# Rotary attention on one Trainium2 core: a unit's second maxima ahead of its second scores on TensorE

## The chip, the cores and the metric

The kernel runs on one core of a Trainium2 chip. The metric is the device time of one execution in microseconds (us). TensorE does the matrix products, VectorE the reductions and elementwise work on them, ScalarE the exponentials and copies, GpSimd smaller elementwise work, and SyncE starts the transfers. Each engine takes its own instructions in order; semaphores hold an instruction until what it needs is there.

## The reference

Two blocks of attention, each followed by a gated feed-forward block, all on layer-normed input and added to it: x has 16 batches of 512 tokens with 128 features. The first attention is causal, the second rotary and not causal. Both have 16 heads of width 8.

```python
x = x + attn_a(layernorm(x))        # causal
x = x + ffn(layernorm(x))
x = x + attn_b(layernorm(x))        # rotary
x = x + ffn(layernorm(x))

# attn_b
q, k = rope(q, k)
scores = einsum('bhnd,bhmd->bhnm', q, k) / sqrt(d)
attn = softmax(scores, axis=-1)
out = einsum('bhnm,bhmd->bhnd', attn, v)
```

## The kernel before

There are four stages with barriers between them: causal attention, feed-forward, rotary attention, feed-forward. The change touches only the program of TensorE inside `attention` (lines 773 to 787), and only what it does for the rotary stage.

Attention is a pipeline over batches, with steps n from -1 to 19. In step n the queries, keys and values of batches n+1 and n are projected, the row maxima of the scores of batch n-1 are found, the scores of batch n-2 are made again with the maxima subtracted and put through the exponential, and the weighted values of batches n-2 and n-3 and the output projection of batch n-4 are done. Scores and maxima of both kinds meet in the 15 steps from n = 2 to n = 16.

A step is 16 units u. A unit holds four score matrices of 128 keys by 512 queries, two for each of two pairs of heads:

- `scores(n, u, 0)` and `scores(n, u, 1)` (line 681) are two matmuls each, one on the lower and one on the upper half of the rows, into the banks of `ps_score`. ScalarE reads each bank with an exponential (line 662) and writes `b_prob`.
- `maxes(n, 2u)` and `maxes(n, 2u+1)` (line 695) are two matmuls each, into two of the four banks of `ps_max`. VectorE reduces the two banks to negated maxima in one instruction (line 577).
- `weigh` (line 716) multiplies the probabilities of the unit two before with the values: four products into `ps_out`. ScalarE copies the output of a group of four units to `b_o_raw` (line 635).
- `misc_work` holds what comes once in a step: the projections of keys (in unit 0), turned keys (2), values (4), output (6), queries (11) and turned queries (13) into `ps_max` (lines 733, 769, 745), and into `ps_score` the turned maxima (1 and 10, line 725) and the turned input (9, line 753). VectorE and ScalarE take the results out in the unit after.

Banks go round in a fixed order that is worked out from the lists `act_turns` and `dve_turns`. `ps_score` has three banks: a score may start when the exponential of the score three turns earlier has read its bank (`act_bank_free`). In a unit without other work the second matmul of the first scores so waits for the first exponential of the second scores of the unit before. `ps_max` has two pairs of banks: maxima may start when VectorE has read what was put there two turns earlier (`dve_banks_free`). Where another projection has taken a turn, the next unit's first maxima wait for the second reduction of this unit, not for the first.

VectorE works through its list in order too: in the unit after a projection it takes that result out before the unit's two reductions. The statistics of the normalisation (lines 180, 184) stand ahead of the reductions of unit 6, the reciprocals and the output projection's sum (lines 607, 613) ahead of those of unit 7, the normalised input (line 202) ahead of those of unit 8.

Of the kernel before, what the change touches and what calls it, by code (L numbers as in the profile page):

```python
# [55 lines left out]
def count(per, b, more=0):  # L56

    return per * b + more


def wait(eng, sem, value):

    if isinstance(value, int) and value <= 0:
        return
    eng.wait_ge(sem, value)
# [141 lines left out]
def attention(nc, sem, m, a, tag, causal):  # L207
# [3 lines left out]
    rotary = not causal  # L211
# [37 lines left out]
    def width(j):  # L249

        return P * j if causal else 0

    def on(n, lag):

        return 0 <= n - lag < B
# [23 lines left out]
    def dve_banks(name, k=0):  # L279

        i = 2 * (dve_at[name, k] % 2)
        return m["ps_max"][:, i:i + 2]
# [26 lines left out]
    def dve_banks_free(pe, n, name, k=0):  # L309

        before = turn_before(dve_turns, 2, n, dve_at[name, k])
        if before is None:
            return
        name, b, k = before
        if name == "max":
            pe.wait_ge(s["max"], count(MAXES, b, k + 1))
        elif name == "proj":
            pe.wait_ge(s["resid"], b + 1)
        elif name == "v":
            pe.wait_ge(s["v"], b + 1)  # L320
        elif name in ("qr", "kr"):
            pe.wait_ge(s[name[0] + "_turn"], b + 1)
        else:
            pe.wait_ge(s[name + "_main" if rotary else name], b + 1)
# [10 lines left out]
    with own, nc.Block() as block:  # L335
# [195 lines left out]
        def _(dve):  # L531
            dve.wait_ge(s["loads"], 80 if rotary else 64)

            def split_weights():

                dve.wait_ge(s["w_raw"], 16 * len(W_PIECES))
                for i, (_, name, cols) in enumerate(W_PIECES):
                    at = slice(W_AT[name], W_AT[name] + cols)
                    full = raw(i).rearrange("p k f -> p (k f)")
                    dve.tensor_copy(m["w_hi"][:, at], full).then_inc(s["w_hi"], 1)  # L540
                    dve.wait_ge(s["w_hi"], i + 1)
                    dve.tensor_tensor(m["w_lo"][:, at], full, m["w_hi"][:, at].bitcast(F32), ALU.subtract)\
                        .then_inc(s["w_lo"], 1)
                    dve.wait_ge(s["w_lo"], i + 1)
                    dve.tensor_reduce(m["w_rest"][:, i:i + 1], m["w_lo"][:, at].bitcast(F32), AX.X, ALU.max,
                                      apply_absolute_value=True).then_inc(s["w_rest"], 1)
# [119 lines left out]
        def _(pe):  # L666
            pe.wait_ge(s["loads"], 80 if rotary else 64)

            def scores(n, u, half):

                b, c = n - 2, (n - 2) % STACKS
                G, j = u // T, u % T
                p, lo = 2 * G + half, width(j)
                if half == 0 and u % (UNITS // 2) == 0:
                    h = u // (UNITS // 2)
                    pe.wait_ge(s[f"aug{h}"], count(32, b, 32))
                for o in range(2):
                    k = 4 * u + 2 * half + o
                    rows = slice(SIDE * o, SIDE * o + KROWS + AUG)
                    act_bank_free(pe, n, "score", k)  # L680
                    pe.matmul(act_bank("score", k)[:, 0:S - lo], m["stack_k"][c][rows, p, P * j:P * (j + 1)],  # L681
                              m["stack_q"][c][rows, p, lo:S], start=True, stop=True).then_inc(s["score"], 1)

            def maxes(n, k):

                b, c = n - 1, (n - 1) % STACKS
                p, t = k // T, k % T
                if k == 0:
                    pe.wait_ge(s["stack_q"], count(LOADS, b, LOADS))
                    pe.wait_ge(s["stack_k"], count(LOADS, b, LOADS))  # L690
                dve_banks_free(pe, n, "max", k)
                to, keys = dve_banks("max", k), P * (t + 1) if causal else S
                for o in range(2):
                    rows = slice(SIDE * o, SIDE * o + KROWS)
                    last = pe.matmul(to[:, o, 0:keys], m["stack_q"][c][rows, p, P * t:P * (t + 1)],  # L695
                                     m["stack_k"][c][rows, p, 0:keys], start=True, stop=True)
                if causal:
                    for o in range(2):
                        last = pe.matmul(to[:, o, keys - P:keys], m["mask_q"][:], m["ident_b"][:],  # L699
                                         start=False, stop=True, skip_group_check=True)  # L700
                last.then_inc(s["max_ps"], 1)

            def weigh(b, u):

                G, j = u // T, u % T
                if u == 0:
                    pe.wait_ge(s["v_aug"], b + 1)
                if j == 0:
                    wait(pe, s["o_raw"], count(GROUPS, b, G))
                if causal:  # L710
                    pe.wait_ge(s["masked"], count(UNITS, b, u + 1))
                else:
                    pe.wait_ge(s["prob"], count(4 * UNITS, b, 4 * u + 4))
                lo = width(j)
                for g in range(4):
                    last = pe.matmul(m["ps_out"][32 * g:32 * g + HD + 1, lo:S], m["v_aug"][b % 2][:, j, 4 * G + g, :],  # L716
                                     m["prob"][u % PROBS][:, g, lo:S], start=(j == 0), stop=(j == T - 1),
                                     skip_group_check=True)
                last.then_inc(s["pv"], 1)
# [53 lines left out]
            for n in range(-1, STEPS):  # L773
                for u in range(UNITS):
                    if on(n, 2):
                        scores(n, u, 0)
                    if on(n, 1):
                        maxes(n, 2 * u)
                    if u < 2 and on(n, 3):
                        weigh(n - 3, UNITS - 2 + u)  # L780
                    if u >= 2 and on(n, 2):
                        weigh(n - 2, u - 2)
                    if on(n, 2):
                        scores(n, u, 1)
                    if on(n, 1):
                        maxes(n, 2 * u + 1)
                    misc_work(n, u)

# [332 lines left out]
```

## Time and profile before

| what | value |
|---|---|
| time, median of 3 runs (lowest to highest) | 2466.25 us (2465.03 to 2470.92) |
| time of the profiled execution | 2471.75 us |
| its span, from the first to the last instruction | 2470.0 us |
| granted TensorE clock over the span | 0.94 of full speed |
| TensorE busy (matmuls), share of the span | 2097.5 us, 85% |
| VectorE busy | 1723.2 us, 70% |
| ScalarE busy | 1482.2 us, 60% |
| rotary attention, 1238 to 2065 us: busy TensorE, VectorE, ScalarE | 715.03, 683.70 and 592.56 us of 827 |

A busy time is the sum over an engine's instructions, overlaps counted once. In a row of the timeline, the start and the duration of one group of neighbouring instructions of a kind are given (x2 is two of them), and in brackets how long the engine had been idle and what it waited for. Matmuls are pipelined, so a pair can show 0.39 us while the next pair starts 0.22 us after it.

### The profile page before, as it was taken

What the parts mean: (1) busy time and instruction counts of PE and PEld (TensorE: products, weight loads), DVE (VectorE), ACT (ScalarE), POOL (GpSimd) and SP (SyncE); (2) the same over time, 40 slices, a digit from 0 to 9 for tenths busy, and PEclk for the clock granted to TensorE, in tenths of its full rate; (3) what the DMA queues carried; (4) which work ended last, traced back from release to release, by engine and by line L of the source; (5) the groups of instructions that cost most, each with busy time, mean ns of one, the idle gap of its engine ahead of it and who ended that gap; (6) DMA issues with size and microseconds to landing.
All of it is one profiled execution on the core that took longest, in us unless ns stands there. A gap on an engine that the chain in (4) does not pass through costs nothing. (4 is left out here: it accounts for less than half of the span.)

```text
span 2470.0 us, 37314 instructions
## 1 busy us (share of the span) xinstructions
PE 2097.5 (85%) x13378; PEld 971.9 (39%) x13378; DVE 1723.2 (70%) x2590; ACT 1482.2 (60%) x2980; POOL 982.3 (40%) x1184
## 2 busy tenths in 40 slices
PE   0799999999985999998378898989898885999998
PEld 0233333333322777776112222222222112777776
DVE  5677777777643667664388889888988843666663
ACT  0166666666662655655037777777777773655655
POOL 2355555555421544544322332233323101554544
PEclk8599999999985999999569999999999997999999
DMA  5535454545310000000433344334433300000000
GB/s 155 108 78 103 83 106 88 105 85 106 67 21 11 1 1 1 1 1 2 101 77 62 68 86 87 68 67 88 85 70 65 64 16 11 9 9 14 13 10 18
DMA packets 99853, 136.48 MB, mean 55 GB/s; under 512 B 20560, under 2 KB 81488, under 8 KB 93520
## 3 DMA queue, kind: packets, MB, share of 16 engines
q1 hardware_dynamic: 99664, 134.02, 26.0%
q8 instruction: 111, 1.82, 0.3%
q14 instruction: 78, 0.64, 0.1%
HBM read 67.91 MB, written 55.57 MB: 50 GB/s over the span
## 5 line engine op out<-in xcount | busy, mean ns | idle before, releaser
L577 DVE TENSOR_REDUCE b_negmax<-ps_max 128x2 f32<-128x1024 f32 x512 | 614.2, 1221 | 92.9 <-PE ps_max L695 91.5
L662 ACT ACTIVATE b_prob<-ps_score 128x512 f32<-128x512 f32 x1024 | 545.8, 599 | 206.7 <-PE ps_score L681 205.5
L662 ACT ACTIVATE a_prob<-ps_score 128x512 f32<-128x512 f32 (+3 forms) x1024 | 384.0, 437 | 226.0 <-PE ps_score L681 224.0
L577 DVE TENSOR_REDUCE a_negmax<-ps_max 128x2 f32<-128x256 f32 (+3 forms) x512 | 411.4, 822 | 150.1 <-PE ps_max L699 142.6
L681 PE MATMUL ps_score<-b_stack_q,stack_k 50*128 50x512 bf16 x1024 | 258.8, 387 | 56.8 <-ACT b_prob L662 48.3
L716 PE MATMUL ps_out<-b_prob,b_v_aug 128*9 128x512 f32 x2048 | 268.6, 596 | 17.7 <-ACT b_o_raw L635 11.6
L978 PE MATMUL ps_score<-fb_h,w_hi 128*128 128x512 f32 x1024 | 252.0, 401 | 29.7 <-DVE fb_h L892 28.7
L978 PE MATMUL ps_score<-fa_h,w_hi 128*128 128x512 f32 x1024 | 251.4, 400 | 29.7 <-DVE fa_h L892 28.7
L494 POOL TENSOR_SCALAR_AFFINE_SELECT a_prob<-a_prob 128x512 f32<-128x512 f32 x256 | 162.0, 635 | 276.8 <-ACT a_prob L662 276.8
L695 PE MATMUL ps_max<-stack_k,b_stack_q 48*128 48x512 bf16 x1024 | 231.1, 397 | 27.1 <-DVE b_negmax L577 17.3
L681 PEld LDWEIGHTS ps_score<-b_stack_q,stack_k 50*128 50x128 bf16 x1024 | 63.9, 93 | 417.8 <-ACT b_prob L662 337.3
L978 PEld LDWEIGHTS ps_score<-fb_h,w_hi 128*128 128x128 f32 x1024 | 193.3, 190 | 82.7 <-DVE fb_h L892 36.6
L978 PEld LDWEIGHTS ps_score<-fa_h,w_hi 128*128 128x128 f32 x1024 | 193.0, 190 | 82.4 <-DVE fa_h L892 36.6
L716 PE MATMUL ps_out<-a_prob,a_v_aug 128*9 128x512 f32 (+3 forms) x2048 | 195.9, 456 | 27.3 <-ACT a_o_raw L635 17.1
L681 PE MATMUL ps_score<-a_stack_q,stack_k 50*128 50x512 bf16 (+3 forms) x1024 | 199.4, 315 | 9.7 <-ACT a_prob L662 6.4
L695 PE MATMUL ps_max<-stack_k,a_stack_q 48*128 48x128 bf16 (+3 forms) x1024 | 173.5, 312 | 17.8 <-DVE a_negmax L577 10.6
L452 POOL TENSOR_TENSOR b_qf<-b_qf,b_turned 128x512 f32<-128x512 f32 x32 | 40.6, 1268 | 356.4 <-DVE b_turned L565 356.4
L681 PEld LDWEIGHTS ps_score<-a_stack_q,stack_k 50*128 50x128 bf16 x1024 | 63.0, 93 | 230.2 <-ACT a_prob L662 124.8
L699 PE MATMUL ps_max<-ident_b,mask_q 128*128 128x128 bf16 x1024 | 150.8, 231 | 0.0
L846 POOL TENSOR_TENSOR fb_h<-fb_h2f,fb_h 128x512 fp32r<-128x512 f32 x64 | 82.6, 1290 | 144.5 <-ACT fb_h L931 144.5
L846 POOL TENSOR_TENSOR fa_h<-fa_h2f,fa_h 128x512 fp32r<-128x512 f32 x64 | 82.6, 1290 | 144.0 <-ACT fa_h L931 144.0
L202 DVE TENSOR_SCALAR xhat<-x,mv,rstd 128x128 f32<-128x128 f32 x256 | 112.4, 501 | 19.2 <-POOL rstd L194 19.2
(139 smaller groups left out, 2877.1 us busy)
## 6 DMA issues: line engine op xcount, KB each, us to landing
stack_k<-d_stack SPq DMA_DIRECT2D x64, 384.0 KB, 6.0
d_stack<-a_parts SPq DMA_DIRECT2D x64, 192.0 KB, 2.8
a_stack_q<-d_stack SPq DMA_DIRECT2D x32, 384.0 KB, 5.7
d_stack<-b_parts SPq DMA_DIRECT2D x64, 192.0 KB, 2.8
b_stack_q<-d_stack SPq DMA_DIRECT2D x32, 384.0 KB, 5.6
d_stack<-a_parts SPq DMA_DIRECT2D x64, 128.0 KB, 2.8
d_stack<-b_parts SPq DMA_DIRECT2D x64, 128.0 KB, 2.8
d_stack<-a_parts SPq DMA_DIRECT2D x64, 64.0 KB, 2.5
```

What stands on the lines that cost most here:

```text
L202: last = dve.tensor_scalar(m["xhat"][:, t, :], m["x"][:, b, t, :], m["mv"][:, t, 0:1], m["rstd"][:, t:t + 1], ALU.subtract, ALU.mult)
L452: pool.tensor_tensor(m["qf"][:, i], m["qf"][:, i], m["turned"][:, i], ALU.add).then_inc(s[name], 1)
L494: pool.affine_select(out=tri, in_=tri, compare_op=ALU.is_ge, fill=0.0, base=0, pattern=[[0, 4], [1, P]], channel_multiplier=-1).then_inc(s ...
L577: dve.tensor_reduce(m["negmax"][:, t, :, p], dve_banks("max", k)[:, :, 0:keys], AX.X, ALU.max, negate=True).then_inc(s["max"], 1)
L662: act.activation(m["prob"][u % PROBS][:, g, lo:S], act_bank("score", 4 * u + g)[:, 0:S - lo], ACT.Exp).then_inc(s["prob"], 1)
L681: pe.matmul(act_bank("score", k)[:, 0:S - lo], m["stack_k"][c][rows, p, P * j:P * (j + 1)], m["stack_q"][c][rows, p, lo:S], start=True, st ...
L695: last = pe.matmul(to[:, o, 0:keys], m["stack_q"][c][rows, p, P * t:P * (t + 1)], m["stack_k"][c][rows, p, 0:keys], start=True, stop=True)
L699: last = pe.matmul(to[:, o, keys - P:keys], m["mask_q"][:], m["ident_b"][:], start=False, stop=True, skip_group_check=True)
L716: last = pe.matmul(m["ps_out"][32 * g:32 * g + HD + 1, lo:S], m["v_aug"][b % 2][:, j, 4 * G + g, :], m["prob"][u % PROBS][:, g, lo:S], sta ...
L846: pool.tensor_tensor(h[k][:, 1, f], hf[k][:, f % 2], h[k][:, 0, f], ALU.subtract)\
L978: mm = pe.matmul(to, w[:, cols], moving(part), start=first and i == 0, stop=last and i == len(pairs) - 1)
```

## The change

In TensorE's loop over units the call that makes the second maxima of a unit moves, for the rotary stage, ahead of the call that makes the second scores. In the causal stage the order stays. Everything else is as before.

```diff
                     if u >= 2 and on(n, 2):
                         weigh(n - 2, u - 2)
+                    if rotary and on(n, 1):
+                        maxes(n, 2 * u + 1)
                     if on(n, 2):
                         scores(n, u, 1)
-                    if on(n, 1):
+                    if causal and on(n, 1):
                         maxes(n, 2 * u + 1)
                     misc_work(n, u)
```

## Rows read from the trace of the kernel before

**Rows 1.** Busy time by engine (start:end, us, then PE to POOL, clock, DMA).
```profile
1565.20:1614.70 49.50, 44.54 (x292) 10.96 (x292) 44.20 (x52) 37.07 (x71) 14.93 (x20) 1.00 0.38 77
```

**Rows 2.** Waits in the same step: total us, times, longest.
```profile
PEld ps_score L681 <- ACT b_prob L662: 20.6, 29, 0.9
...
DVE b_negmax L577 <- PE ps_max L695: 5.4, 17, 0.7
...
PE ps_score L681 <- ACT b_prob L662: 2.6, 7, 1.0
```

**Rows 3.** Timeline of TensorE, unit 12 into unit 13, no other work.
```profile
1603.72 1.05 PE L716 MATMUL ps_out<-b_prob,b_v_aug 128*9 128x512 f32 x8
1604.69 0.39 PE L681 MATMUL ps_score<-b_stack_q,stack_k 50*128 50x512 bf16 x2
1604.92 0.38 PE L695 MATMUL ps_max<-stack_k,b_stack_q 48*128 48x512 bf16 x2
1605.14 0.38 PE L681 MATMUL ps_score<-b_stack_q,stack_k 50*128 50x512 bf16 x1
1605.77 0.39 PE L681 MATMUL ps_score<-b_stack_q,stack_k 50*128 50x512 bf16 x1 [0.25 <-ACT b_prob L662]
1605.77 0.60 PE L695 MATMUL ps_max<-stack_k,b_stack_q 48*128 48x512 bf16 x2
1606.30 1.05 PE L716 MATMUL ps_out<-b_prob,b_v_aug 128*9 128x512 f32 x8
```

**Rows 4.** Timeline of VectorE and ScalarE in that unit.
```profile
1603.91 1.22 DVE L577 TENSOR_REDUCE b_negmax<-ps_max 128x2 f32<-128x1024 f32 x1
...
1605.35 2.36 DVE L577 TENSOR_REDUCE b_negmax<-ps_max 128x2 f32<-128x1024 f32 x2 [0.22 <-PE ps_max L695]
...
1605.12 2.06 ACT L662 ACTIVATE b_prob<-ps_score 128x512 f32<-128x512 f32 x4 [0.49 <-PE ps_score L681]
```

**Rows 5.** Timeline, unit 11 with the projection of the queries into unit 12.
```profile
1601.69 0.38 PE L695 MATMUL ps_max<-stack_k,b_stack_q 48*128 48x512 bf16 x2
1602.00 1.13 PE L733 MATMUL ps_max<-b_xT,b_weights 128*128 128x512 f32 x2
1603.06 0.39 PE L681 MATMUL ps_score<-b_stack_q,stack_k 50*128 50x512 bf16 x2
1603.40 0.39 PE L695 MATMUL ps_max<-stack_k,b_stack_q 48*128 48x512 bf16 x2
...
1602.11 1.23 DVE L577 TENSOR_REDUCE b_negmax<-ps_max 128x2 f32<-128x1024 f32 x1 [0.29 <-PE ps_max L695]
```

**Rows 6.** Timeline, unit 6 with the statistics and the output projection.
```profile
1584.37 0.86 DVE L180 BATCH_NORM_STATS2 stats<-x 128x6 f32<-128x128 f32 x4
...
1585.56 2.32 DVE L577 TENSOR_REDUCE b_negmax<-ps_max 128x2 f32<-128x1024 f32 x2
...
1586.90 1.13 PE L745 MATMUL ps_max<-b_weights,b_oT 128*128 128x128 f32 x8 [0.69 <-DVE b_negmax L577]
```

**Rows 7.** Timeline, unit 1 with the turned maxima into unit 2.
```profile
1570.43 1.08 ACT L662 ACTIVATE b_prob<-ps_score 128x512 f32<-128x512 f32 x2 [0.49 <-PE ps_score L681]
1571.40 0.57 ACT L627 ACTIVATE b_nm_rows<-ps_score 16x512 bf16<-16x512 bf16 x1
1571.87 0.57 ACT L635 ACTIVATE b_o_raw<-ps_out 128x512 f32<-128x512 f32 x1
...
1572.54 1.04 PE L716 MATMUL ps_out<-b_prob,b_v_aug 128*9 128x512 f32 x8 [0.37 <-issue]
```

**Rows 8.** Timeline, units 8 and 9 behind the normalised input; group output of unit 14.
```profile
1592.28 4.62 DVE L577 TENSOR_REDUCE b_negmax<-ps_max 128x2 f32<-128x1024 f32 x4
...
1593.14 0.39 PE L681 MATMUL ps_score<-b_stack_q,stack_k 50*128 50x512 bf16 x1 [0.25 <-ACT b_prob L662]
1593.57 0.39 PE L695 MATMUL ps_max<-stack_k,b_stack_q 48*128 48x512 bf16 x2
...
1608.68 0.60 ACT L635 ACTIVATE b_o_raw<-ps_out 128x512 f32<-128x512 f32 x1
```

## The prediction, made before the change was run

> **What bounds the kernel now.** I read the page first for where the time lies, then the 16 units of one step of the rotary attention (49.50 us, the same from step to step), first by engine, then by who waits for whom, then in order of time. In that step TensorE is busy for 44.54 us, VectorE for 44.20 and ScalarE for 37.07 [rows 1]. No engine is full, so the length of a step must come from a chain that goes over several engines. Two waits are candidates. VectorE waits 17 times for the maxima, 5.4 us in all; TensorE waits 7 times for ScalarE's exponentials before a score, 2.6 us, and its weight loads 29 times, 20.6 us [rows 2]. The change helps the first kind, and I must see what it does to the second.
>
> The unit without other work shows it [rows 3, 4]. The probabilities are weighed from 1603.72, the second scores start at 1604.69 (0.97 later), ScalarE takes up their exponential at 1605.12 (0.43 later), and the second matmul of the next unit's first scores, which writes the bank that this exponential reads, starts at 1605.77 (0.65 later). The next weighing starts at 1606.30, another 0.53 later. The sum 0.97 + 0.43 + 0.65 + 0.53 = 2.58 us is the distance from weighing to weighing, with nothing left over. So this unit is held by a loop: weighing, second scores, exponential, bank free, next first scores, weighing. I call it the score loop. VectorE sits beside it: it starts its reductions at 1603.91 and 1605.35, and after a start it could begin the next 1.13 us later (two back to back take 2.36, one 1.23) [rows 4]. It waits for the second maxima and doesn't set the pace here.
>
> **What the change moves.** Nothing is added or taken away: the same two matmuls per unit, with their bank wait, now stand before the second scores instead of behind them, in the 15 steps that have both (one batch's scores, the next batch's maxima). No DMA, no instruction of another engine and no bank assignment changes. The moved wait is for the reduction of the unit before, or for the operation that takes out another result; both ended long before the weighing does (the reduction begun at 1603.91 ends at 1605.14, its bank is next wanted after 1606.3) [rows 4], so I price it at nothing. If it were late, the second scores would now be queued behind it, and ScalarE behind them.
>
> *The score loop gets longer.* From the start of the second scores to the start of the second maxima it is 0.23 us [rows 3]. In the new order that time lies between the weighing and the second scores, in the middle of the loop. TensorE's idle time later in the unit can't give it back, because that idle time is itself the wait for the exponential, which has moved by the same 0.23. So a unit held by the score loop goes from 2.58 to 2.81 us. How many are there? Of the 7 waits of matmuls for exponentials, six are this pattern (0.25 us each) and one is the step's first score (1.0) [rows 2, 3]. Three more boundaries, behind the turned maxima and the turned input, have the same chain with one more ScalarE operation in it: two exponentials from 1570.43, row of maxima at 1571.40, output of a group at 1571.87, and the next weighing at 1572.54 waits for that [rows 7]. That is ten. One of them doesn't count: behind the normalisation the first maxima wait for VectorE's reduction (started at 1592.28, over at 1593.51) until 1593.57, while the score that waited for the exponential starts at 1593.14: 0.43 us of slack [rows 8]. A second is unit 5, ahead of the output projection, which is taken with it below. Eight remain: 8 x 0.23 = +1.84 us in a step.
>
> *Units held by VectorE get shorter.* Here another result is computed at the unit's end, and the next first maxima wait until the second reduction has left the bank. In the unit with the projection of the queries the reduction starts at 1602.11 and the first maxima at 1603.40, 1.29 later; the first scores had started at 1603.06 and need 0.22 of TensorE, so 0.12 us is waiting [rows 5]. The second maxima come 0.23 sooner after the weighing, the reduction too (its 0.22 of idle time goes, and VectorE was free); but TensorE, busy with scores, can use only 0.12. Four units are of this kind (keys, turned keys, values, queries): -0.48. For the turned queries nothing: with the wait gone the next weighing waits for the output of a group, which ScalarE starts at 1608.68 behind the last exponential [rows 8], and that is 0.23 later now.
>
> *Statistics and output projection.* Behind the second reduction of unit 5 stand the statistics (from 1584.37), then two reductions from 1585.56, and the projection at 1586.90 waits for the first of them, 0.69 us idle [rows 6]. That is one chain of VectorE over two units. It starts with a reduction that the change frees by 0.22, so two units together shorten by 0.22. TensorE reaches the projection only about 0.2 later than before, inside the 0.69.
>
> The sum for a step: 1.84 - 0.48 - 0.22 = +1.14 us. The last two of the 15 steps lack the queries of a next batch; I count them like the others. 15 x 1.14 = 17 us. The profiled execution then goes from a span of 2470.0 to 2487.0 and from 2471.75 to 2488.75 us; the median of the runs shown is 5.5 below that execution, so 2466.25 + 17 = 2483 us, +0.7%.
>
> The one term that the trace of before does not show is what a pair of maxima costs between a weighing and a pair of scores. Below: nothing, if it ran beside the weighing's tail or the scores; it can't gain. Above: 0.31 us, the distance from the second maxima to the next kind of matmul (1601.69 to 1602.00) [rows 5]. I take 0.23, the distance between a pair of scores and the pair of maxima behind it, since both are pairs of matmuls of 512 columns on the two halves of the rows [rows 3]. The ends give 15 x (0 - 0.70) = -10 and 15 x (8 x 0.31 - 0.70) = +27 us: 2456 to 2493.
>
> **Rivals.** *VectorE sets the pace (faster).* If the score loop had slack that I don't see, the reductions would come sooner and everything would follow. For it: VectorE is busy for 89% of the step and has 5.4 us of idle time in front of the maxima, 0.22 us of it in front of the second reduction of the plain unit [rows 1, 2, 4]. If the 0.22 went in all 16 units, that would be 15 x 16 x 0.22 = 53 us: 2413. In the small form only the units held by VectorE gain and the loop costs nothing: -10 us, 2456. The small form is the likelier of the two. It decides for the change if the second score's bank is free without the exponential's being late. Against it: the loop closes to 0.01 us [rows 3, 4]. The Trainium skill ("Perfetto Trace Analysis", Optimization Strategy) tells one to take the most contended engine, find the gaps on it and make what they wait for start sooner. By occupancy, with TensorE's judged otherwise, that engine is VectorE, and this change does what the rule asks; by that rule the time would fall. The rows of the score loop speak against it.
>
> *The loop takes only half (no change).* If the pair of maxima overlaps the scores behind it by half, a step changes by 8 x 0.12 - 0.70 = +0.3 us, 4 us in all: 2470. The trace shows for pairs only full distances of 0.22 to 0.23, against it.
>
> *It takes more (slower still).* If the weight loads of the second scores no longer hide, 0.31 in the eight loops, and none of the 0.70 is given back because the exponential then holds those units too, it is 15 x 8 x 0.31 = 37 us: 2503. Against it: where another result is computed, TensorE works for 1.06 us between the second maxima's 0.31 and the next scores [rows 5], which is longer than the 0.65 from exponential to score.
>
> *It changes nothing* because the order isn't what the text says: the loop in the code is plain, 1%, taken into the rival of no change.
>
> **How the numbers follow.** Within 0.3% (7.4 us, about what a measurement of this kernel can tell from no change) is 2458.9 to 2473.6. My forecast, 2474 to 2495 around 2483, has 0.73; the half cost 0.12; the faster rival 0.09 (part of its small form lies under 2458.9, part in the band; I leave 0.08 faster and put 0.01 in the band); slower still 0.06. So faster 0.08, same 0.13, slower 0.79. The range leaves out 0.17: the faster rival, some of the band and most of the slowest; 2466 to 2496.
>
> **What the profile after would show.** In the unit without other work: weighing, maxima 0.97 later, second scores at 1.20, exponential at 1.63, next weighing at 2.81. The step at 50.6 to 50.7 us instead of 49.50, VectorE's busy time as before (44.2) and its idle time larger, though the wait in front of the second reduction is smaller and now stands in front of the first. ScalarE's wait for the scores grows by about 1 us a step. The unit pair with the statistics is shorter by 0.2. The other three stages and their times are the same. The prediction is wrong if the plain unit stays at 2.58 (the pair hides), or if the weighings' distances in units with other work don't fall.

## The result, and the profile after

In the first four runs the changed kernel took 2490.74 us (median, 2488.13 to 2494.15) and the kernel before 2465.64 us; the ratio is 1.0097, 95% interval 1.0083 to 1.0112. Six more runs against 23 of the kernel before (below) give 1.0074, 1.0057 to 1.0092: 18 us slower. I had forecast 2483 us and 17 us slower; the interval of the first four runs (20 to 28 us) leaves that out, the later one (14 to 23 us) holds it. The profiled execution took 2489.67 us with a span of 2487.9 us, 17.9 us over the span before.

One step of the rotary attention in the kernel after, by engine, and its waits (us in total, times, longest). The stretch is again one step, from the first score of a batch to that of the next.

```profile
1574.80:1625.40 50.60, 43.92 (x292) 10.88 (x293) 44.78 (x51) 36.96 (x71) 14.94 (x20) 1.00 0.37 75
```

```profile
ACT b_prob L662 <- PE ps_score L681: 13.6, 22, 0.8
...
DVE b_negmax L577 <- PE ps_max L695: 5.1, 9, 0.9
PE ps_score L681 <- ACT b_prob L662: 4.8, 9, 1.3
```

The clock is at 1.00 and the busy times are those of [rows 1] within 0.62 us. VectorE's rose from 44.20 to 44.78, though one reduction takes 1221 ns in the mean as before (1222). VectorE waits for maxima 9 times where it waited 17 times, and yet as long as before, 5.1 us against 5.4 [rows 2]. The change removed VectorE's wait in front of the second maxima in most units, and the time came back in longer waits in front of the first. TensorE's matmuls wait for exponentials 4.8 us where it was 2.6 [rows 2].

Units 12 and 13, the stretch of [rows 3], on TensorE, and then VectorE and ScalarE in unit 12 as in [rows 4]:

```profile
1613.72 1.05 PE L716 MATMUL ps_out<-b_prob,b_v_aug 128*9 128x512 f32 x8
1614.69 0.39 PE L695 MATMUL ps_max<-stack_k,b_stack_q 48*128 48x512 bf16 x2
1614.92 0.59 PE L681 MATMUL ps_score<-b_stack_q,stack_k 50*128 50x512 bf16 x3
1615.99 0.39 PE L681 MATMUL ps_score<-b_stack_q,stack_k 50*128 50x512 bf16 x1 [0.47 <-ACT b_prob L662]
1615.99 0.60 PE L695 MATMUL ps_max<-stack_k,b_stack_q 48*128 48x512 bf16 x2
1616.52 1.05 PE L716 MATMUL ps_out<-b_prob,b_v_aug 128*9 128x512 f32 x8
```

```profile
1613.95 2.40 DVE L577 TENSOR_REDUCE b_negmax<-ps_max 128x2 f32<-128x1024 f32 x2
...
1616.63 2.53 DVE L577 TENSOR_REDUCE b_negmax<-ps_max 128x2 f32<-128x1024 f32 x2 [0.28 <-PE ps_max L695]
...
1615.34 2.06 ACT L662 ACTIVATE b_prob<-ps_score 128x512 f32<-128x512 f32 x4 [0.59 <-PE ps_score L681]
```

The two reductions of the unit now stand back to back (one row, x2, from 1613.95), so the wait of 0.22 us inside the pair is gone; in its place VectorE waits 0.28 us ahead of the next pair. ScalarE's exponential starts 1.62 us after the weighing (1.40 before), TensorE idles 0.47 us for it and not 0.25, and the next weighing comes after 2.80 us, not 2.58.

The output projection, as in [rows 6], and the next weighing behind the turned maxima, as in [rows 7]:

```profile
1593.83 0.86 DVE L180 BATCH_NORM_STATS2 stats<-x 128x6 f32<-128x128 f32 x4
...
1596.36 1.13 PE L745 MATMUL ps_max<-b_weights,b_oT 128*128 128x128 f32 x8 [0.25 <-DVE b_negmax L577]
...
1581.55 0.57 ACT L635 ACTIVATE b_o_raw<-ps_out 128x512 f32<-128x512 f32 x1
...
1582.22 1.05 PE L716 MATMUL ps_out<-b_prob,b_v_aug 128*9 128x512 f32 x8 [0.37 <-issue]
```

The projection's wait fell from 0.69 to 0.25 us. In unit 2 the weighing still follows the copy of the output by 0.67 us, so it moved with it.

### The profile page after: what moved, and what is told of

It reads as the page before. It is cut to its first block and busy times, and to the rows that moved or that the text cites. A ratio compares the mean times of both kernels' runs of the same rounds, so it can differ in the third digit from the quotient of the medians.

```text
span 2487.9 us, 37314 instructions
## 1 busy us (share of the span) xinstructions
PE 2090.7 (84%) x13378; PEld 971.6 (39%) x13378; DVE 1731.7 (70%) x2590; ACT 1480.7 (60%) x2980; POOL 982.4 (39%) x1184
## 5 line engine op out<-in xcount | busy, mean ns | idle before, releaser
L577 DVE TENSOR_REDUCE b_negmax<-ps_max 128x2 f32<-128x1024 f32 x512 | 616.5, 1221 | 97.1 <-PE ps_max L695 89.9
L681 PE MATMUL ps_score<-b_stack_q,stack_k 50*128 50x512 bf16 x1024 | 240.6, 383 | 90.7 <-ACT b_prob L662 84.7
L695 PEld LDWEIGHTS ps_max<-stack_k,b_stack_q 48*128 48x128 bf16 x1024 | 51.4, 94 | 252.9 <-issue 108.7
```

Source lines behind the costliest of these rows:

```text
L577: dve.tensor_reduce(m["negmax"][:, t, :, p], dve_banks("max", k)[:, :, 0:keys], AX.X, ALU.max, negate=True).then_inc(s["max"], 1)
```

## The experiments

All lengths of a step below are the distance between the first scores of two steps in one profile. In the kernels before and after these rows are:

```profile
1565.26 0.39 PE L681 MATMUL ps_score<-b_stack_q,stack_k 50*128 50x512 bf16 x2 [1.04 <-ACT b_prob L662]
...
1614.76 0.39 PE L681 MATMUL ps_score<-b_stack_q,stack_k 50*128 50x512 bf16 x2 [1.05 <-ACT b_prob L662]
```

```profile
1574.83 0.39 PE L681 MATMUL ps_score<-b_stack_q,stack_k 50*128 50x512 bf16 x2 [1.26 <-ACT b_prob L662]
...
1625.42 0.39 PE L681 MATMUL ps_score<-b_stack_q,stack_k 50*128 50x512 bf16 x2 [1.26 <-ACT b_prob L662]
```

That is 49.50 and 50.59 us.

**The change timed again (change_again).** The first four runs stood 25 us apart by their medians, the steps explain 17.6.

> The change itself, timed in more rounds to see whether the median moves as far as the steps do. The profile of the changed kernel has 50.59 us for a step against 49.50, 17.6 us over the 15 steps. If the score loop explains all of it, the median difference is 17 to 18 us (ratio 1.007). If something outside the rotary steps is slower too, it is 21 to 28 us (1.0083 to 1.011) as in the first four runs, and the profile must show it in another stage.

Measured: 2488.29 us (6 runs) against 2469.83 (23 runs), ratio 1.0074, 1.0057 to 1.0092, 18 us. The steps are 50.59 us again. From the first score of step 2 to that of step 17 it is 757.5 us here and 759.3 in the first profile of the changed kernel, against 741.7 in the kernel before: 15.8 and 17.6 us. So the steps account for the change within about 2 us. The first four runs had, by chance, the kernel before 4 us under its median here and the changed kernel 2 us over.

The 1.8 us between the two profiles are in the first of the 15 steps (53.25 and 51.45 us), which isn't like the others. TensorE's granted clock was still 0.50 of full speed, its lower level (1.2 GHz), for the first 5 to 15 us of it in all profiles. In both_ends below this lasted 5.5 us and the step took 47.78 us, 0.2 more than the next; in loop_again it lasted 14.5 us and the step took 54.76 us, 4.0 more than the next. Sums over the 15 steps of two profiles carry this difference, the distances of the steps behind it don't.

**Only where VectorE holds TensorE (only_held).** From the kernel before:

```diff
+                    early = rotary and u in (0, 2, 4, 5, 7, 11)
+                    if early and on(n, 1):
+                        maxes(n, 2 * u + 1)
                     if on(n, 2):
                         scores(n, u, 1)
-                    if on(n, 1):
+                    if not early and on(n, 1):
                         maxes(n, 2 * u + 1)
```

> The second maxima go ahead of the second scores only in units 0, 2, 4, 5, 7 and 11, whose reduction releases something that TensorE or VectorE waits for. Score loop theory: the loop isn't lengthened where it binds, the gains stay: 3 x 0.12 + 0.09 + 0.22 (unit 5, through the statistics) + 0.20 (unit 7, through the normalised input) = 0.87 us a step, a step of 48.6, 13 us faster in all (2453). Rival, a pair of maxima ahead of scores costs TensorE time wherever it stands: 6 x 0.23 = 1.4 us a step slower or, less the gains, 0.5 slower.

Measured: 2462.67 us (12 runs), ratio 0.9977, 0.9963 to 0.9991: 6 us faster. The step:

```profile
1558.54 0.39 PE L681 MATMUL ps_score<-b_stack_q,stack_k 50*128 50x512 bf16 x2 [1.05 <-ACT b_prob L662]
...
1607.38 0.39 PE L681 MATMUL ps_score<-b_stack_q,stack_k 50*128 50x512 bf16 x2 [1.05 <-ACT b_prob L662]
```

That is 48.84 us, 0.66 less than before and not 0.87. The missing 0.2 is unit 7: from its weighing to that of unit 8 it grew from 2.59 to 2.81, and from unit 8 to unit 9 it fell from 2.80 to 2.59. The score loop took what the normalised input gave. The other terms came as written. The steps give 9 us, the runs 6; the last experiment bears on the rest.

**Only where the score loop holds (only_loop).** The same edit with units (1, 3, 9, 10, 12, 14, 15).

> The second maxima go ahead of the second scores only in units 1, 3, 9, 10, 12, 14 and 15, where the next unit waits for the exponential of the second scores. Score loop theory: 7 x 0.23 = 1.6 us a step slower and nothing gained, a step of 51.1, 24 us slower in all (2490): more than the whole change costs. Rival, VectorE sets the pace: no slower than before, since its waits in front of the second reductions shrink in these units too.

Measured: 2504.04 us (4 runs), ratio 1.0143, 1.0121 to 1.0166: 35 us slower, more than the whole change. The step is 51.02 us (1570.99 to 1622.01):

```profile
1570.99 0.39 PE L681 MATMUL ps_score<-b_stack_q,stack_k 50*128 50x512 bf16 x2 [1.26 <-ACT b_prob L662]
...
1622.01 0.39 PE L681 MATMUL ps_score<-b_stack_q,stack_k 50*128 50x512 bf16 x2 [1.26 <-ACT b_prob L662]
```

This is +1.52 a step, 7 x 0.22, as the loop has it, and 22 us in 15 steps. The rest isn't in the steps. The second maxima came sooner after the weighing in seven units here, and nothing was gained by it: no distance between weighings fell, and VectorE's waits for maxima rose from 5.4 to 6.3 us in the longer step. That strikes out the rival that VectorE sets the pace.

**The other end of the loop (first_inside).** From the kernel before, with `scores` and `maxes` able to make one of their two matmuls alone or to take the upper rows first:

```diff
+                    between, ahead = both and u in (4, 8, 11, 13, 15), both and u in (0,)
+                    if ahead:
+                        maxes(n, 2 * u)
                     if on(n, 2):
-                        scores(n, u, 0)
-                    if on(n, 1):
-                        maxes(n, 2 * u)
+                        scores(n, u, 0, (0,) if between else (0, 1))
+                    if on(n, 1) and not ahead:
+                        maxes(n, 2 * u, (1, 0) if between else (0, 1))
+                    if between:
+                        scores(n, u, 0, (1,))
```

> The other end of the loop, from the kernel before: in units 4, 8, 11, 13 and 15 the first maxima (upper rows, then lower) go between the two first scores, where TensorE waits for the exponential, and in unit 0 ahead of both. The second maxima stay where they were. Score loop theory: 0.22 us of TensorE's work leaves the loop, and the weighing follows the score by 0.31 and not 0.53; the plain unit falls from 2.58 to 2.36; in unit 8 the normalised input binds and nothing is gained; 5 x 0.22 = 1.1 us a step faster, a step of 48.4, 16 us faster in all (2449). Rival, VectorE sets the pace: no change, for its wait in front of the second reduction stays.

Measured: 2459.72 us (12 runs), ratio 0.9961, 0.9945 to 0.9977: 10 us faster. The steps account for 15 of the 16 us that were forecast; the last experiment bears on the rest. The step is 48.51 us, 0.99 less and not 1.1: the five units gave 0.22 each, but from weighing to weighing units 4 and 13 grew by 0.11 together. Units 12 and 13:

```profile
1594.47 1.05 PE L716 MATMUL ps_out<-b_prob,b_v_aug 128*9 128x512 f32 x8
1595.45 0.39 PE L681 MATMUL ps_score<-b_stack_q,stack_k 50*128 50x512 bf16 x2
1595.67 0.38 PE L695 MATMUL ps_max<-stack_k,b_stack_q 48*128 48x512 bf16 x2
1595.89 0.38 PE L681 MATMUL ps_score<-b_stack_q,stack_k 50*128 50x512 bf16 x1
1595.94 0.55 PE L695 MATMUL ps_max<-stack_k,b_stack_q 48*128 48x512 bf16 x2
1596.52 0.39 PE L681 MATMUL ps_score<-b_stack_q,stack_k 50*128 50x512 bf16 x1
1596.84 0.62 PE L716 MATMUL ps_out<-b_prob,b_v_aug 128*9 128x512 f32 x4
```

The score still follows the second scores by 1.07 us (1.08 before [rows 3]), the exponential's time; the weighing follows the score by 0.32 and not 0.53. From weighing to weighing it is 2.37. Taking a pair out of the loop gives 0.21 as putting one in costs 0.22.

**The cost doubled, behind and ahead (twice_behind, twice_ahead).** In the kernels before and after, the pair of second maxima is computed twice into the same banks:

```diff
-                for o in range(2):
+                for o in (0, 1, 0, 1) if rotary and k % 2 and on(n, 2) else (0, 1):
```

> From the kernel before, its order kept: the pair of second maxima is computed twice in the 15 steps, in its place behind the second scores. The work of TensorE grows by 16 x 0.22 = 3.5 us a step. Score loop theory: behind the scores the pair falls into time in which TensorE waits for the exponential. The plain unit stays at 2.58; only what hangs on the reduction moves (units 0, 2, 4, 11, 13, the chains of units 5 and 7: 7 x 0.22, and 0.1 for the turned input), a step of 51.1. Rival, TensorE's work counts wherever it stands: a step of 53.0, plain unit 2.80.

> The same doubling in the changed kernel, where the pair stands ahead of the second scores: the suspected cost doubled. Score loop theory: all of it counts, nearly everywhere, since the units that VectorE held have used up their slack: plain unit 2.81 + 0.22 = 3.03, a step of 50.6 + 15 x 0.22 = 53.9. The same added work costs 1.6 us a step behind the scores and 3.3 ahead of them. Rival, TensorE's work counts wherever it stands: both grow by the same.

Measured, one run each: 2492.43 and 2533.77 us. Units 12 and 13 of each, behind first:

```profile
1612.62 1.05 PE L716 MATMUL ps_out<-b_prob,b_v_aug 128*9 128x512 f32 x8
1613.60 0.39 PE L681 MATMUL ps_score<-b_stack_q,stack_k 50*128 50x512 bf16 x2
1613.83 0.60 PE L695 MATMUL ps_max<-stack_k,b_stack_q 48*128 48x512 bf16 x4
...
1615.21 1.05 PE L716 MATMUL ps_out<-b_prob,b_v_aug 128*9 128x512 f32 x8
```

```profile
1629.23 1.05 PE L716 MATMUL ps_out<-b_prob,b_v_aug 128*9 128x512 f32 x8
1630.21 0.61 PE L695 MATMUL ps_max<-stack_k,b_stack_q 48*128 48x512 bf16 x4
1630.65 0.59 PE L681 MATMUL ps_score<-b_stack_q,stack_k 50*128 50x512 bf16 x3
1631.72 0.39 PE L681 MATMUL ps_score<-b_stack_q,stack_k 50*128 50x512 bf16 x1 [0.47 <-ACT b_prob L662]
...
1632.26 1.05 PE L716 MATMUL ps_out<-b_prob,b_v_aug 128*9 128x512 f32 x8
```

The same four matmuls (x4) leave the unit at 2.59 us behind the scores and make it 3.03 ahead of them. The steps are 51.06 us (+1.56 on the kernel before) and 53.83 (+3.24 on the changed one). Expected were 51.1 and 53.9. So it is the place in the loop that costs, not the work.

**Both gains together (both_ends).** The edits of only_held and of first_inside in one kernel.

> The two edits that gained, together: second maxima early in units 0, 2, 4, 5, 7 and 11, first maxima inside or ahead of the first scores in units 0, 4, 8, 11, 13 and 15. If they add: 49.50 - 0.66 - 0.99 = 47.85 us a step, 24 us over the 15 steps, and a little more since unit 8 can now gain (0.2 a step). If VectorE becomes the bound, less: its busy time of 44.2 us and gaps leave about 3.5 us. The time over all depends on the clock in the last scores-only steps too, which fell to half for 17 to 41 us in the last three profiles and not in the kernel before: 2443 us if it stays up, up to 2455 if it falls.

Measured: 2445.15 us (6 runs) against 2468.64 (11 runs), ratio 0.9909, 0.9890 to 0.9929: 23 us faster than the kernel before. The step is 47.79 us (1552.69 to 1600.48):

```profile
1552.69 0.39 PE L681 MATMUL ps_score<-b_stack_q,stack_k 50*128 50x512 bf16 x2 [0.48 <-ACT b_prob L662]
...
1600.48 0.39 PE L681 MATMUL ps_score<-b_stack_q,stack_k 50*128 50x512 bf16 x2 [0.48 <-ACT b_prob L662]
```

The two gains add within 0.06 us (0.66 + 0.99 = 1.65, found 1.71). That small difference is itself a sum: units 7 and 8, whose distances from weighing to weighing neither edit alone had shortened as a pair (5.39 us before), fell to 5.25, 0.14 of the further 0.2; unit 4 lost the 0.09 that only_held had gained there (3.30 us, 3.23 before).

**The clock after the steps (both_filled, loop_again, held_again, before_again, held_filled).** Three profiles had a longer last stretch than the others, from the first exponential of step 17, the step with scores only, to the last residual. Two kernels here, both_filled with the order of both_ends and held_filled with that of only_held, fill that step with a pair of matmuls in each unit whose result nobody reads:

```diff
+                    if rotary and n == B + 1:
+                        filler(u)
                     misc_work(n, u)
```

> The same with one more pair of matmuls in each unit of the step with scores only (n = 17), behind the second scores, into banks of the maxima that nobody reads: work that is thrown away. It asks whether the clock falls there for want of work on TensorE. If it does, the granted clock stays at 1.00 from the last maxima to the last weighing, the stretch from the first exponential of step 17 to the last residual takes 59 to 60 us as in the kernel before (73, 66 and 66 in the last three profiles), and the times of the runs lie closer together, 6 us or more under both_ends. If the clock falls for another reason, nothing changes or it is slower.

> A second profile of only_loop, whose times lay 34 us over the kernel before while its steps explain 22. If the clock's fall in the stretch after the steps (65.6 us instead of 59.1 there) belongs to this order of work, it shows again; if it is chance, the stretch takes 59 us and the execution is about 6 us shorter.

> A second profile of only_held, whose stretch after the steps took 73.1 us with the clock at half for 41 us. The same question: again about 73 us if it belongs to the kernel, 59 to 66 if it is chance.

> A second profile of the kernel before. Its steps must be 49.50 us again. If the clock's fall after the steps is chance in every kernel, it may show here too (stretch of 66 or 73 us instead of 59.1).

> The order of only_held, with one more pair of matmuls in each unit of the step with scores only, its result thrown away: the filling of both_filled, tried where the clock did fall. If want of work on TensorE lets it fall, the stretch after the steps takes 59 us and the median is some 6 to 10 us under that of only_held (2462.67); if not, the clock falls as before and the times are those of only_held.

The stretch in the kernel before, in only_held, in held_again and in held_filled (busy times by engine, then granted clock, DMA):

```profile
2008.60:2067.80 59.20, 37.08 (x234) 9.96 (x226) 2.39 (x5) 36.33 (x70) 4.07 (x5) 0.89 0.12 21
```

```profile
1996.70:2069.80 73.10, 53.10 (x234) 10.80 (x226) 2.35 (x5) 36.34 (x70) 4.07 (x5) 0.65 0.09 17
```

```profile
1996.80:2062.90 66.10, 45.40 (x234) 10.11 (x228) 2.35 (x5) 36.44 (x70) 4.08 (x5) 0.77 0.10 18
```

```profile
1993.90:2053.10 59.20, 40.30 (x266) 10.52 (x258) 2.34 (x4) 36.34 (x70) 4.07 (x5) 0.91 0.11 21
```

In the first three the same instructions took 59 to 73 us, and the granted clock goes with it, 0.89 down to 0.65. The stretch was long in every profile of only_held (73, 66), only_loop (66, 67) and first_inside (66), and 59 to 61 us in both profiles of the kernel before, both of the change, and one each of twice_behind, twice_ahead and both_ends. before_again took 2466.2 us and had 59.2 us there. loop_again took 2497.88 us with a long stretch again, held_again 2466.76. In the kernel before, the clock fell to its lower level only 47 us into the stretch, when the last weighings were over; in only_held, only_loop and first_inside it fell 8 to 29 us into it. What TensorE did just before doesn't tell them apart: here are 10 us of the kernel before, where the clock stayed up, and the same 10 us of first_inside, 9 us before it fell.

```profile
2018.00:2028.00 10.00, 7.99 (x56) 2.29 (x53) 0.70 (x2) 8.39 (x17) 0.55 (x1) 1.00 0.29 53
```

```profile
2000.00:2010.00 10.00, 7.99 (x56) 2.29 (x54) 0.72 (x2) 8.37 (x17) 0.84 (x1) 1.00 0.28 53
```

A stretch longer by 7 us fits first_inside (15 us gained in the steps, 10 in the runs) and brings only_loop from 22 to 29 of its 35 us; about 6 us of it stay without a row. For only_held it fits less well: 9 us from the steps less 7 or 14 would leave 2 us or a loss, and the runs gave 6. Both of its profiled executions (2473.05 and 2466.76 us) are slower than its median of 2462.67, so its other runs need not all have the long stretch; only profiled executions show it.

Filling: both_filled took 2445.65 us (6 runs, ratio 0.9899, 0.9880 to 0.9919), no different from both_ends, whose clock hadn't fallen either. held_filled took 2456.38 us (6 runs, ratio 0.9965, 0.9952 to 0.9978) where only_held had 0.9977, and its clock stayed up. In both_filled, too, the runs lay no closer together (10 us from the lowest to the highest, 12 in both_ends). held_filled speaks for want of work as the cause, but the two intervals overlap and it is one profile against two; it isn't settled. Nor do I know whether the order of work in the steps before decides it, or how.

## Why the prediction was right

*The score loop.* Right, and it carries the result. The plain unit went from 2.58 to 2.80 us (forecast 2.81), with the exponential 1.62 after the weighing (1.63). The eight units at 0.23 measured 0.21 to 0.23 each. Taking the loop's units alone, taking a pair out at its other end, and doubling the pair in and outside it all moved the step by the number of 0.22s that the loop says (within 0.11 us a step). One row for it stood in the trace of before and I didn't use it: in step 17, without maxima, the weighings are 2.37 us apart, the loop less the first maxima.

```profile
2019.11 1.05 PE L716 MATMUL ps_out<-b_prob,b_v_aug 128*9 128x512 f32 x8
2020.09 0.60 PE L681 MATMUL ps_score<-b_stack_q,stack_k 50*128 50x512 bf16 x3
2021.16 0.39 PE L681 MATMUL ps_score<-b_stack_q,stack_k 50*128 50x512 bf16 x1 [0.47 <-ACT b_prob L662]
2021.48 1.05 PE L716 MATMUL ps_out<-b_prob,b_v_aug 128*9 128x512 f32 x8
```

*The units held by VectorE.* Right: keys, turned keys and queries each fell from 3.23 to 3.11 us between weighings (0.12), the values from 3.23 to 3.14. The turned queries gained nothing, since the output's copy took the reduction's place, as forecast.

The weighing that starts the unit with the queries, before and after (the next ones are at 1603.72 [rows 3] and, above, 1613.72):

```profile
1600.48 1.05 PE L716 MATMUL ps_out<-b_prob,b_v_aug 128*9 128x512 f32 x8
```

```profile
1610.61 1.05 PE L716 MATMUL ps_out<-b_prob,b_v_aug 128*9 128x512 f32 x8
```

*Statistics and projection.* Right: units 5 and 6 together went from 6.90 to 6.68 us, -0.22. The projection's wait fell by 0.44 (0.69 to 0.25): half is the reduction that ended sooner, half TensorE's later arrival, as forecast. The weighings around the two units, before and after:

```profile
1581.60 1.04 PE L716 MATMUL ps_out<-b_prob,b_v_aug 128*9 128x512 f32 x8
...
1588.50 1.05 PE L716 MATMUL ps_out<-b_prob,b_v_aug 128*9 128x512 f32 x8
```

```profile
1591.28 1.05 PE L716 MATMUL ps_out<-b_prob,b_v_aug 128*9 128x512 f32 x8
...
1597.96 1.05 PE L716 MATMUL ps_out<-b_prob,b_v_aug 128*9 128x512 f32 x8
```

*The sum.* +1.14 us a step forecast, +1.09 measured in the second to the thirteenth of the 15 steps. The last two, which lack the statistics, the normalised input and the queries of a next batch, grew by 1.56 and 1.24 us (from 48.20 each to 49.76 and 49.44): units 5 and 6 together grow by 0.13 there and don't shorten by 0.22, and unit 8, without the normalised input, grows by 0.22 too. I had counted them like the others, 0.5 us too little, and the 0.05 too much in each of the other steps made up for it, which is luck. With the first step at 1.09 the 15 come to 13 x 1.09 + 2.80 = 17.0 us for 17; the two profiles, whose first steps differ, have 17.6 and 15.8. The price of the pair, the term without a row, came out at the 0.23 that I took from the neighbouring pair and at neither end.

*The rivals.* VectorE as the pace is out (only_loop). Half the cost is out (0.22 in each loop). The slower form is out: the second scores follow the maxima by 0.23 us and not 0.31, and the units held by VectorE did give their part back. The Trainium skill ("Perfetto Trace Analysis", Optimization Strategy) says to find the gaps on the engine that one optimizes for and to make what they wait for start sooner. Read by occupancy, as in the prediction, this would have made the kernel faster; here the measurement decides against it. VectorE was busy for 89% of the step, its second maxima came 0.23 us sooner after the weighing, and the step grew by 2%.

*What was too small.* I didn't see that the time outside the steps moves by itself by more than the 0.3% in question, nor the clock's part in it, in the first of the steps too. And in only_held I gave unit 7 a gain of 0.2 although the score loop of the next unit stood 0.2 behind it: the same look at what is late next, missed once.

## What to carry to other kernels

Before you move work on an engine, add up the distances round each loop that goes over two engines (work, result, bank free, next work). Where they close to the period with nothing over, that loop is the pace, and anything put between its parts costs its full time even if the engine idles elsewhere in the loop. Put the work of others into the loop's waiting time instead. Here the first maxima went in front of the matmul that waits for its bank, which gave 0.4%; together with early second maxima where VectorE holds the unit it was 0.9%, where the change lost 0.7%. An engine that is busy for 89% of the time with gaps in front of it is not the bound by that alone.

## What the runs showed of the hardware that I had not expected

In a stretch with the same instructions the granted TensorE clock was 0.89 in the kernel before and 0.65 to 0.77 in only_held, only_loop and first_inside, which differ from it only in the order of work ahead of the stretch. It made the stretch 7 to 14 us longer, as much as the edits themselves. That the order decides it isn't shown: both_ends, with the edits of two of the three, kept its clock.

Doubling a pair of matmuls of 48 x 512 on the two halves of the rows costs 0.22 us for the pair, not for each, where it couldn't hide (twice_ahead): from the maxima at 1630.21 to the scores at 1630.65 there are 0.44 us for four matmuls.
